# A 16-head attention stage on one core: skewed head loop, query weights loaded per head, keys begun between other products

## The reference, cut to what matters

```python
q = rms(split(layernorm(x) @ Wq)) * gq       # 16 heads of 128
k = rms(split(ctx @ Wk)) * gk
v = split(ctx @ Wv)
x = x + g_xattn[1] * (softmax(q @ k.T / sqrt(128)) @ v) @ Wo
```

## Time and profile before

| what | value |
|---|---|
| median of 3 runs | 1154.46 us (1153.31 to 1155.91) |
| the profiled execution | 1153.1 us |
| its span, first to last instruction | 1151.4 us |
| instructions | 16015 |
| TensorE busy | 862.6 us (75%) |
| VectorE busy | 728.3 us (63%) |
| ScalarE busy | 568.6 us (49%) |
| GpSimd busy | 409.8 us (36%) |
| mean granted TensorE clock | 0.882 |

### The profile page before, as it was taken

How to read it: one execution, slowest core, us unless ns; L and a number is a source line. 1 busy time by engine, 2 the same in 40 slices (tenths; PEclk the granted TensorE clock), 3 DMA queues, 4 the chain that set the end, 5 groups by cost and what they waited for, 6 DMA issues and landing times. The chain is left out here.

```text
span 1151.4 us, 16015 instructions
## 1 busy us (share of the span) xinstructions
PE 862.6 (75%) x5130; PEld 498.6 (43%) x5130; DVE 728.3 (63%) x1415; ACT 568.6 (49%) x1075; POOL 409.8 (36%) x307
## 2 busy tenths in 40 slices
PE   4465666879799999999498466988629999823477
PEld 1122224532466666666276351222415666512235
DVE  5799997897555555555678656787451333147686
ACT  3443343558577666766365354777413333213153
POOL 0576640399234333343132180000012666202122
PEclk7589998999899999999799795899958999956579
DMA  3222107300000000000000101300191332230001
GB/s 88 75 77 82 60 1 275 128 1 1 1 1 0 0 1 1 0 0 0 5 1 1 51 1 38 111 21 2 52 387 55 64 62 47 32 96 1 0 1 37
DMA packets 35626, 53.41 MB, mean 46 GB/s; under 512 B 5144, under 2 KB 26400, under 8 KB 35568
## 3 DMA queue, kind: packets, MB, share of 16 engines
q1 hardware_dynamic: 29072, 44.53, 11.4%
q0 software_dynamic: 4416, 6.03, 3.2%
q10 hardware_dynamic: 2080, 2.10, 0.5%
HBM read 46.09 MB, written 6.49 MB: 46 GB/s over the span
## 5 line engine op out<-in xcount | busy, mean ns | idle before, releaser
L1170 POOL TENSOR_TENSOR a_scratch<-a_scratch,a_inverse 128x512 f32<-128x512 f32 x64 | 66.5, 1039 | 163.3 <-DVE a_inverse L1282 163.3
L2086 DVE TENSOR_REDUCE a_tops<-bank 128x4 f32<-128x1024 f32 x64 | 77.9, 1225 | 28.2 <-PE bank L1784 25.8
L323 PE MATMUL bank<-ssm_seen,ident 128*128 128x512 f32 x128 | 64.1, 625 | 37.2 <-DVE ssm_seen L499 37.2
L425 POOL TENSOR_TENSOR ssm_drive<-ssm_du,ssm_b_row 128x1024 f32<-128x1024 f32 x32 | 75.1, 2350 | 33.5 <-DVE ssm_state L489 33.4
L2285 PE MATMUL bank<-wup,moe_xT 128*128 x184 | 85.7, 610 | 1.2 <-ACT moe_xT L2343 1.1
L1939 ACT ACTIVATE wup<-bank,a_exp_scale 128x1024 f32<-128x1024 f32 x64 | 70.9, 1112 | 25.5 <-PE bank L1804 25.1
L391 ACT ACTIVATE bank<-ssm_delta,ssm_a_neg 128x510 f32<-128x510 f32 x64 | 44.1, 689 | 79.1 <-DVE ssm_state L489 77.7
L489 DVE TENSOR_TENSOR_SCAN ssm_state<-bank,ssm_drive 128x512 f32<-128x512 f32 x64 | 74.8, 1210 | 7.5 <-POOL ssm_drive L425 4.9
L2515 DVE TENSOR_TENSOR moe_act_f<-bank,moe_silu 128x512 f32<-128x512 f32 x23 | 15.9, 692 | 96.7 <-ACT moe_silu L2350 85.0
L1095 ACT ACTIVATE a_scratch<-bank,a_bias,a_q_factor 128x256 f32<-128x256 f32 x128 | 70.9, 560 | 11.8 <-DVE a_bias L1269 9.0
L1262 DVE TENSOR_REDUCE a_bias<-bank 128x2 f32<-128x512 f32 x64 | 44.1, 689 | 50.2 <-PE bank L936 49.8
(11 more groups left out here) (475 smaller groups left out, 2237.7 us busy)
## 6 DMA issues: line engine op xcount, KB each, us to landing
ssm_b_row<-ssm_b_spill SPq DMA_DIRECT2D x16, 512.0 KB, 3.6
wup<-in_l_up_dram SPq DMA_DIRECT2D x8, 1024.0 KB, 8.3
wdn<-in_l_down_dram SPq DMA_DIRECT2D x8, 512.0 KB, 9.4
keys<-in_l1x_o_dram SPq DMA_DIRECT2D x1, 2048.0 KB, 12.2
X<-in_x_dram SPq DMA_DIRECT2D x1, 1024.0 KB, 6.8
lora_raw<-in_l_gate_dram SPq DMA_DIRECT2D x1, 1024.0 KB, 8.4
lora_raw<-in_l_up_dram SPq DMA_DIRECT2D x1, 1024.0 KB, 10.4
keys<-in_l_down_dram SPq DMA_DIRECT2D x1, 1024.0 KB, 12.5
```

The source lines that it names most:

```text
L323: last = pe.matmul(bank[:, 4 + 2 * k + h, :], core.ident[:, :], seen[:, k, h * HALF:(h + 1) * HALF], start=False, stop=m >= STEPS - CC, sk ...
L425: pool.tensor_tensor(drive[:, k, :], du[:, k, :], b_row[:, n % NROW, :], ALU.mult).then_inc(S["drive_ready"], 1)
L1170: pool.tensor_tensor(prob[:, j, :, :], prob[:, j, :, :], inverse[:, j, :].unsqueeze(2).to_broadcast([P, 2, SEQ]), ALU.mult).then_inc(S["p_ ...
L2086: dve.tensor_reduce(tops[:, f // 2 % 3, :, first:first + 2].rearrange("p q h -> p h q"), bank[:, at:at + 2, :].rearrange("p h (q n) -> p h ...
```

## The change

The change touches `hold_keys`, `stage_lora_moe` and `stage_attention_16`.

In the expert stage the GpSimd subtractions and the write-back of scaled sources are gone; ScalarE casts key weights and transposed context after its loop, all three powers of two come from one ones-product and one chain, and of the third ternary matrix only the scaling is done there. Its rounding and bounding stand in the attention stage.

In the attention stage the low halves of the context and the first half of the key weights are VectorE's first work after the small scales, which wait for the gains' load, in front of the norm. TensorE begins the keys after four of the eight `Wv Wo` groups and alternates the two; x is turned later, in two halves. The context's high half is made by ScalarE. The power of two of `Wv Wo` comes behind the fourth pair of heads. Query weights have no fp16 copy of all heads any more: for each unit SP loads a head's 128x256 f32 into one of two buffers, GpSimd makes its high half and VectorE its low half, two units ahead. The last pair's key scaling is done inside the first unit. In the head loop mix 0 and output 0 of a head come one step later than before, and scores 1 earlier; ScalarE does both exponentials before the high half of the first; the residual add is split by j.

```diff
                 act.wait_ge(half_in[3], 16)
-                weigh(core.wq_in, wq_spare, 0, NTOK, q_sizes[:, 0:1])
+                weigh(core.wq_in, 2, 0)
+                weigh(core.wq_in, 2, 1)
             if t == 4:
+                weigh(core.wq_in, 2, 2)
+                weigh(core.wq_in, 2, 3)
+                act.preload_act_table_set("sqrt_and_others")
+            if t == 6:
                 act.wait_ge(sized, 1)
-                act.activation(core.half_power[:, 0:2], size[:, 0:2], ACT.Sqrt, scale=2.0 ** 40).then_inc(rooted, 1)
-                for k in range(1, 3):
-                    weigh(core.wq_in, wq_spare, k, NTOK, q_sizes[:, k:k + 1])
-            if t == 5:
-                weigh(core.wq_in, wq_spare, 3, NTOK, q_sizes[:, 3:4])
-                act.wait_ge(half_ready, 1)
-                high(core.wk_half, core.wk_in, 0, 0)
-            if t == 6:
-                high(core.wk_half, core.wk_in, 0, 1)
-                act.wait_ge(half_in[1], 16)
-                high(core.ctxT_half, core.ctxT_in, 1, 0)
-            if t == 7:
-                act.wait_ge(sized, 2)
-                act.activation(core.half_power[:, 2:3], size[:, 2:3], ACT.Sqrt, scale=2.0 ** 40).then_inc(rooted, 1)
+                act.activation(core.half_power[:, :], size[:, :], ACT.Sqrt, scale=2.0 ** 40).then_inc(rooted, 1)
+        act.wait_ge(half_ready, 1)
+        act.wait_ge(half_in[1], 16)
+        high(ctxT_flat, core.ctxT_in, 1, 0)
+        for k in range(2):
+            high(wk_flat, core.wk_in, 0, k)
...
         pool.memset(wR[:, :, :], 0.0).then_inc(padded, 1)
-        for n, (halves, src, k) in enumerate(((core.wk_half, core.wk_in, 0), (core.wk_half, core.wk_in, 1),
-                                              (core.ctxT_half, core.ctxT_in, 0))):
-            cols = slice(k * NTOK, (k + 1) * NTOK)
-            pool.wait_ge(half_hi, n + 1)
-            pool.tensor_tensor(part(halves, 1)[:, cols], src[:, cols], part(halves, 0)[:, cols], ALU.subtract)
+        pool.memset(sizes[:, :], 0.0).then_inc(sizes_clear, 1)
...
+            if t in (5, 6):
+                rounded(t - 5)
+            if t in (6, 7):
+                bounded(t - 6)
             if t == 7:
-                dve.wait_ge(sizes_out, 1)
-                dve.tensor_reduce(size[:, 2:3], bank[:, 7, 0:4], AX.X, ALU.add).then_inc(sized, 1)
-            if 4 <= t < 7:
-                i = t - 4
-                chain(dve.tensor_scalar(raw[i][:, :], raw[i][:, :], wscale[:, i:i + 1], ROUND, ALU.mult, ALU.add))
-            if 5 <= t < 8:
-                i = t - 5
-                chain(dve.tensor_scalar(raw[i][:, :], raw[i][:, :], ROUND, 1.0, ALU.subtract, ALU.min))
-            if 6 <= t < 8:
-                i = t - 6
-                dve.tensor_scalar(core.tern[i][:, :], raw[i][:, :], -1.0, None, ALU.max)
+                half_scales()
         add(NT - 2)
-        half_scales(slice(2, 3), 2)
+        scaled(2)
         add(NT - 1)
-        dve.tensor_scalar(core.tern[2][:, :], raw[2][:, :], -1.0, None, ALU.max)
...
+        def load_q(h, p):
+            sp.dma_start(wq_in[:, p, :].rearrange("p (c n) -> p c n", c=DC),
+                         d["l1x_q"][bass.ds(h, 1)].rearrange("h (c p) n -> p (h c) n", p=P)).then_inc(wq_loaded[p], 16)
+
+        for p in range(2):
+            load_q(p, p)
         sp.dma_start(gains[:, :], d["l1x_gains"]).then_inc(in_s, 16)
+        for m in range(2):
+            with sp.Fori(1 - m, NH // 2) as i:
+                for p in range(2):
+                    sp.wait_ge(S["wq_split"], 2 * i + (NH * m + p - 1))
+                    load_q(2 * i + p, p)
...
             if n < RING:
-                pe.wait_ge(S["xn_split"], n + 1)
+                pe.wait_ge(S["wk_split"], 2)
...
         def queries(n, m, p):
 
+            pe.wait_ge(S["wq_split"], n + 1)
...
-        for n in range(4):
+        for g in range(4):
+            out_weights(g)
+        for n in range(3):
             keys_of(n)
-        pe.wait_ge(S["vo_topped"], 1)
-        pe.wait_ge(S["xn_split"], 4)
-        pe.wait_ge(S["vo_ready"], PAIRS)
-        pe.matmul(bank[:, 3, 0:1], core.ones[:, :], vo_top[:, :], start=True, stop=True).then_inc(S["vo_sum"], 1)
+        out_weights(4)
...
+        keys_of(3)
+        out_weights(6)
+        out_weights(7)
+        keys_of(4)
+        keys_of(5)
+        turn_xn(0)
+        sums_of(0)
+        keys_of(6)
+        keys_of(7)
+        turn_xn(1)
         pe.wait_ge(consts, 6)
-        for g in range(1, PAIRS):
+        for g in range(2, PAIRS):
+            if g == 4:
+                pe.wait_ge(S["wk_split"], 3)
             keys_of(4 * g)
-            if g >= 2:
-                spread_of(g - 2)
-            else:
-                pe.wait_ge(S["vo_scaled"], 1)
+            if g == 2:
+                pe.wait_ge(S["xn_split"], 4)
+            spread_of(g - 2)
             keys_of(4 * g + 1)
             keys_of(4 * g + 2)
+            if g == 4:
+                pe.wait_ge(S["vo_step"], 5)
             sums_of(g - 1)
             keys_of(4 * g + 3)
+            if g == 3:
+                pe.wait_ge(S["vo_topped"], 1)
+                pe.wait_ge(S["k_logs"], 3)
+                pe.matmul(bank[:, 7, 0:1], core.ones[:, :], vo_top[:, :], start=True, stop=True).then_inc(S["vo_sum"], 1)
...
+            if first and n == NH:
+                pe.wait_ge(S["added"], j + 1)
...
             scores(n, m, p, 0)
+            if before is not None:
+                mix(n - 1, before, 0)
+                turn(n - 1, 1)
             turn_factor(n, p)
-            if before is not None:
-                turn(n - 1, 1)
+            scores(n, m, p, 1)
             if after is not None:
                 queries(n + 1, after, 1 - p)
             if before is not None:
                 mix(n - 1, before, 1)
-            scores(n, m, p, 1)
+                out(n - 1, before, 0)
             turn(n, 0)
             if before is not None:
                 out(n - 1, before, 1)
-                out(n - 1, before, 0)
             if after is not None:
                 query_sums(n + 1, 1 - p)
-            mix(n, m, 0)
 
         pe.wait_ge(S["k_brought"], 4 * PAIRS)
         pe.wait_ge(S["k_logs"], PAIRS)
-        pe.wait_ge(S["key_ready"], 4 * PAIRS)
         pe.wait_ge(S["c_split"], 1)
         unit(0, 0, 0, None, 0)
+        pe.wait_ge(S["key_ready"], 4 * PAIRS)
...
+        for g in range(4):
+            bring_vo(g)
         act.wait_ge(S["backs"], 2)
-        for g in range(PAIRS):
-            if g == 1:
-                act.wait_ge(S["c_split"], 1)
+        bring_keys(0)
+        s.norm_root_half(act, 0)
+        bring_keys(1)
+        bring_keys(2)
+        s.norm_root_half(act, 1)
+        act.preload_act_table_set("natural_log_exp_and_others")
+        bring_vo(4)
+        bring_vo(5)
...
+        xn_high(0)
+        xn_high(1)
+        factors(0)
+        bring_keys(6)
+        bring_keys(7)
+        xn_high(2)
+        xn_high(3)
+        act.activation(c_flat[0], core.ctx_nat[:, :], ACT.Copy, scale=core.half_scale[:, 1:2]).then_inc(S["c_hi"], 1)
...
-                act.wait_ge(S["wq_split"], 4)
+                act.wait_ge(S["wk_split"], 3)
+            if g == 7:
+                act.wait_ge(S["tern_done"], 1)
             for k in range(3):
...
+            if g >= 4:
+                vo_high(g - 4)
...
+                mix_high(n - 1, 0)
                 high_part(n - 1, 1)
             exps(n, p, 0)
             if after:
                 queries(n + 1, 1 - p)
             if before:
                 mix_high(n - 1, 1)
+            exps(n, p, 1)
             high_part(n, 0)
-            exps(n, p, 1)
             if after:
                 query_factor(n + 1, 1 - p)
-            mix_high(n, 0)
...
+        def query_high(n, p):
+            pool.wait_ge(wq_loaded[p], 8 * n + (16 - 8 * p))
+            await_count(pool, S["q_done"], n - 1)
+            pool.tensor_tensor(wq[:, p, 0, :], wq_in[:, p, :], core.half_scale[:, 2:3].to_broadcast([P, DC * HD]), ALU.mult
                                ).then_inc(S["wq_hi"], 1)
-        pool.tensor_scalar(c_flat[0], core.ctx_in, core.half_scale[:, 1:2], None, ALU.mult).then_inc(S["c_hi"], 1)
+
+        for p in range(2):
+            query_high(p, p)
...
+        def unit(n, p, after, later):
+            if later:
+                query_high(n + 2, p)
             normalise(n, 0)
...
+        def lower(halves, src, kind, k, done):
+            dve.scalar_tensor_tensor(quarter(halves[1], k), quarter(src, k), core.half_scale[:, kind:kind + 1], quarter(halves[0], k),
+                                     ALU.mult, ALU.subtract).then_inc(done, 1)
+
+        def query_low(n, p):
+            dve.wait_ge(S["wq_hi"], n + 1)
+            dve.scalar_tensor_tensor(wq[:, p, 1, :], wq_in[:, p, :], core.half_scale[:, 2:3], wq[:, p, 0, :],
+                                     ALU.mult, ALU.subtract).then_inc(S["wq_split"], 1)
+
```

(54 more changed lines are left out.)

226 lines of the change are left out of this document (109 added, 117 removed).

## The result

The changed kernel takes **1124.62 us** (median of 4 runs, 1123.07 to 1126.34); the kernel before took 1154.22 (4 runs, 1153.31 to 1155.91) beside it. The ratio is 0.9742, 95% interval 0.9724 to 0.9761: about 30 us less. Forecast were 1121 us in 1109 to 1134. On a second chip run it took 1124.94 (ratio 0.9745, 0.9720 to 0.9770). Two executions of all that are told of here, one of the kernel before (4209.33 us) and one of E10 (2906.81 us), were in a slower state and stay out of every ratio.

A forecast was written before the change was run, and what follows sets the result against it. A circle through four engines (7.84 us) bound the old head loop, VectorE and GpSimd the keys, VectorE the expert stage's end. Savings 5.5 + 4.9 + 1.4 + 21.3 + 0.5 = 33.6 gave 1121 us, range 1109 to 1134.

The forecast's parts named there:

- Loop: 16-head attention's head loop: unit falls from 7.91 to 7.2 us, 30 intervals give 21.3 us less.
- TensorE's need: Head loop: TensorE's products, summed from their starts in the old order, need 7.1 us per unit, unchanged by the new order.
- Additions per unit: Head loop: each unit's added query load, GpSimd product (0.7 us) and VectorE subtraction (0.4 to 0.5) cost nothing.
- Expert stage: Stage before the keys: work leaves VectorE's tail and ScalarE's casts end it, 5.5 us less, bounds 3.5 and 6.9.
- Keys: Keys stage: VectorE's work plus waits put first scores near 59.9 us after the start instead of 64.8, 4.9 us less.
- First unit: Loop's first unit: goes on at once with four scalings in it, 7.5 us instead of 8.9, 1.4 us less.
- End: End of the head loop: the last add begins half a step earlier, 0.5 us less.
- (a): Head loop: VectorE's query subtraction waits for GpSimd's normalise, unit 7.6 to 7.7 us, time 1134 us; chance 0.17.
- (b): Keys stage: gives nothing because VectorE's waits add up, time 1128 us; chance 0.10.
- (c): Loop and keys: better than forecast, unit 7.05 us and GpSimd's squares bounding the keys, time 1113 us; chance 0.10.
- (d): Head loop: slower, two-slot query buffer makes its own circle, needing a landing of 11.3 us; 1176 us at 12; chance 0.03.
- (e): Whole change: does nothing, a third circle of 7.8 us remains and stages only shift waits, 1154 us; chance 0.02.

The follow-up runs named there:

- E10: Changed kernel with the keys' products put back behind all eight output-weight products, on TensorE and ScalarE: 1127.9 us, ratio 0.9756.
- E3: Changed kernel with each head's query subtraction on VectorE done twice, the extra result going to a spare tile: 1131.3 us, ratio 0.9800.
- E4: Changed kernel with each head's query product on GpSimd done twice, the extra result going to a spare tile: 1125.5 us, ratio 0.9746.
- E11: Changed kernel with TensorE's turn of the query factors made three times into the same place: 1131.0 us, ratio 0.9791.
- E2: Kernel before with the new loop order alone, all query halves still made ahead of the loop: 1134.1 us, ratio 0.9827.
- E8: Changed kernel with the second matrix's last ternary pass on VectorE moved behind the scales in the expert stage: 1123.3 us, ratio 0.9729.
- E5: Changed kernel with VectorE's wait for the gains and their product moved behind its second reduction over the output weights: 1121.4 us, ratio 0.9701.
- E9: Changed kernel with both the edit of E5 and the edit of E8: 1119.7 us, ratio 0.9703.
- E12: The kernel of E9, unedited, measured again on another chip run: 1121.8 us, ratio 0.9706.
- E6: Changed kernel with the context's low half and two query low halves moved behind the output weights' power of two: 1125.7 us, ratio 0.9731.
- E1: Changed kernel with the loop's old order, the wait for all key scalings ahead of the first unit and the joined residual add: 1149.4 us, ratio 0.9926.
- E7: Changed kernel unedited, measured once more on a second chip run: 1124.9 us, ratio 0.9745.

## Why the prediction held, and where it did not

**Loop, 21.3 forecast, 18.6 measured.** TensorE is the bound, as I chose; E3, E4 and E11 show it from three engines. The term that was off is TensorE's need, put at 7.1 from the starts of a unit that waited. The unit without waits, in the timeline above, gives 0.96, 0.66, 0.44, 0.10, 0.87, 1.29, 0.66, 0.66, 0.50, 0.76 and 0.36: 7.26. The scores behind the 32-column sums take 0.96 against 0.87 for those behind the factor turn, the turn between two groups of outputs 0.50 instead of 0.44, the output halves 1.42 instead of 1.40. The 0.49 of a turn in front of an output group stood in the earlier trace rows and was taken as 0.44; scores behind the sums the old order does not have, a mix stands between. My 7.2 was near because I added 0.1 for disturbance, which is luck; the right reason was 0.16 of hand-over on 7.1, and 0.03 in the mean for the odd units of 7.34 and 7.45.

**Additions per unit, nothing forecast.** Right: E2's unit, without them, is no shorter. The product takes 0.80 beside the subtraction (I took 0.7), 0.61 alone; the subtraction 0.47 (0.4 to 0.5). E3 shows the price where the cover goes: 0.8 to 0.9 us in each of two units about the additions.

**Expert stage, 5.5 forecast, 4.9 measured.** It ends on ScalarE's casts as said. The scales end at 220.7 and not at 220.2, because the last hidden product, from which I followed it, comes at 214.31 and not at 213.57; the path behind that product is 5.6 us shorter, as forecast. E8 wins 1.1 more by putting the ternary pass behind the scales.

**Keys, 4.9 forecast, 4.2 measured**, near by errors that cancel. I added VectorE's work, 54.6 us, the gains' wait of 3.1 and 2.2 for the rest, 59.9. Measured are 52.5, 3.7 and 4.4, 60.6. The gains' wait was the right step (E5, E9, E12). But VectorE's sum alone does not bound the stage: it was to be over 90% busy and is 86%, its last three groups wait 2.7 us for TensorE's spreads, and in E6 it stands 4.2 us. What the interleaved keys give is not settled (E10), nor what the last pair's scalings in the first unit give by themselves (E1 takes them back together with the order).

**First unit, 1.4 forecast, 2.15 measured**: 6.77 us from scores to scores at clock 1.00, 7.5 forecast. It is 6.77 or 6.78 in every experiment with the changed loop and prologue but E11. In eight of the experiments a half-clock stretch of 3.4 us fell behind it, and the second unit took 8.7 to 8.9 us (9.1 in E11) instead of 7.20; the changed kernel, E7 and E9 were spared it, which is luck in their traces. **End, 0.5 forecast, 0.6 measured.**

Sum: 18.6 + 4.9 + 4.2 + 2.15 + 0.6 = 30.4, to which my 33.6 compares; the loop's term has 2.7 of the difference. That the profiled executions give 3.6 back behind the attention was in none of my steps; of the medians only 0.8 is missing.

**Rivals.** (a) fell by E3 and E4. The rows agree in kind with the Trainium skill, "SBUF — State Buffer", section "Who interferes with whom", in the keys stage: the 256-column subtraction takes 1.25 us beside squares of 1.22, and they take 0.47 and 1.04 alone. A lock over whole instructions they do not bear out: in E3 both engines begin one every 1.18 us, less than the 0.39 and 1.00 that the two need from start to start alone. In the loop the product loses 0.19 and the subtraction nothing, and both stand where nothing waits. (b) and (c) did not come: the keys gave 4.2, and no unit fell under 7.19. (d): loads land in 1.9 to 3.1 us, far from 11. (e), no gain, fell with the 29.6 us.

## What to carry to other kernels

Read an engine's need from a unit in which it does not wait; a need summed from groups of another order leaves out the passages between groups, here 0.16 of 7.26 us. A load that is used late should be waited for late: moving one wait from the head of a nearly full engine brought the first scores 1.2 us sooner in E5's trace and 3.0 to 3.2 in E9's and E12's, which have E8's edit too. When a sum of one engine's work comes out right, look for its waits all the same: here 2.7 us of them showed a second engine that set the pace at the stage's end. And compare stage by stage: the lengths of stages that no edit touches moved by 2 to 8 us with TensorE's clock.

## What was not expected of the hardware

- The same value products took 107.3, 110.0, 111.25 or 115.3 us, as the granted clock stayed at 0.50 (1.2 GHz) until 13, 22.5, 27 or 42 us after they began, and both kernels that were profiled twice fell on the same length each time. The executions without a profile need not: E5's took 1119.32 to 1122.30 us beside the profiled 1129.90.
- Scores of four float32 products take 0.96 us to the next group's start behind 32-column sums and 0.87 behind a 128-column product; the turn 0.50 between output groups and 0.44 between a mix and the factor turn.
- A 256-column subtraction on VectorE with two inputs in SBUF took 1.25 us beside GpSimd's squares, 2.7 times its 0.47 alone, and they took 1.22 instead of 1.04; the scalings, with one input in PSUM, stayed at 0.74.
